# A graph layer with a gathered neighbour sum, linear attention and two experts: VectorE's large gather-stage steps take one SBUF operand, the last block's own products stand ahead of its last rows, the first expert is requested alone

## The chip, the core and the metric

The kernel runs on one core of one Trainium2 chip. A core has TensorE (PE, with its weight loads shown apart as PEld), VectorE (DVE), ScalarE (ACT), GpSimd (POOL) and SyncE (SP), an SBUF that all of them read, a PSUM of eight banks into which PE writes, and 16 DMA engines. The metric is the device time of one execution in microseconds (us).

## What is computed

```python
xn = layernorm(x)                                  # 12500 rows of 256
agg = segment_sum(xn[src], dst) / max(count, 1)    # 212500 edges, sorted by dst
gnn = relu(agg @ W_l.T + b_l + xn @ W_r.T) + xn
q, k, v = xn@wq+bq, xn@wk+bk, xn@wv+bv             # 8 heads of 32; q, k = elu(.) + 1
attn = (q (k^T v)) / (q . sum(k) + 1e-6) @ wo + bo
x1 = x + gnn + attn
y = layernorm(x1)
out = x1 + layernorm(y + top-2-of-8 experts(y)) * gamma + beta   # one choice for all rows
```

All of it is float32; biases and gains are drawn away from 0 and 1.

## The kernel before, in words

Each engine runs its own hand-ordered program, and they meet at counted semaphores. There are four stages.

**Table.** All rows of x are normalised and written to `xn_table` in HBM as two float16 parts, and the edge lists are turned into index and offset tables.

**Gather stage.** The 12500 output rows are 49 blocks of 256 rows. A block has 34 tiles of 128 edges (the last 29). For each tile POOL issues one indirect DMA that gathers 128 table rows into `msgs`, a ring of one block's tiles; VectorE compares an iota row with the edges' offsets (`one_hots`, L1504) and PE multiplies the one-hot by the gathered rows into a PSUM strip of `pa`. The tiles go in 8 batches per block of 4, 4, 5, 4, 4, 4, 5, 4. POOL may start a batch when ScalarE has copied its indices (`idx_ready`, L738, in ScalarE's order of work) and when PE has used the same batch of the block before (`batch_used`). Strips cover 128 rows and overlap by 64, so ScalarE takes them to SBUF (L768) and VectorE adds the lower and the upper halves of neighbours in `join_strips` (L1513, L1516), and makes a reciprocal count (L1520, L1522). ScalarE scales the joined strips by it (`scale_sums`, L775), and PE turns them (`turn_sums`, L1145).

Beside the gather runs the rest. In blocks 0 to 9 (`shadow_block`, `key_work`) it is the keys: rows turned (L982), `keys` in two halves into two PSUM banks (L995), a bias by VectorE (`add_bias`, L1378), an Exp, the feature map (L1386) and `add_keys` (L1005). In blocks 10 to 19 (`double_block`) two blocks' dense work goes with each gathered block, from block 20 on one (`stage3`; a hardware loop covers most). The dense work of a block: ScalarE normalises the rows (`block_xn`, L762), PE turns them (L1070), ScalarE copies them (L781), PE makes the queries (`queries`, L1078), ScalarE makes exp(q + bq) and q + bq + 1 in four activations (`block_queries`, L790 and L793), VectorE takes min and max (L1548), PE makes the normalizers (L1087), VectorE divides (`normalise_queries`: L1554, L1556, L1558), PE makes the sum's products in `base` (L1105, L1094, L1108, L1109), `mixed_product` and `neighbour_product` (L1094), ScalarE and VectorE finish the row (L800, L1537), its statistics follow, ScalarE makes y (`block_y`, L807), PE turns it (`turn_y`, L1134) and ScalarE keeps it (L815). ScalarE's order in a block's middle is: queries, `block_y`, then the index copies of batches 3 and 4 of the next block.

**Routing.** The mean of y gives the logits; a chain of tiny VectorE steps finds both experts, then SP reads the two numbers and requests W1, b1 and W2 of each.

**Experts.** Weights and y are split in a high and a low part; per quad of 512 rows PE runs `layer1` (L1275) and `layer2` (L1290).

## Time and profile before

| | |
|---|---|
| runs, median of 3 | 3372.62 us (3365.61 to 3381.5) |
| the profiled execution's own time | 3382.15 us |
| its span | 3380.7 us |
| mean granted TensorE clock | 0.809 of full speed |
| busy: PE, POOL, DVE, ACT | 2141.0, 1607.6, 1423.6, 955.7 us |
| gathers | 1661 indirect DMAs |

The profiled execution is 1.45 us longer than its span, and its span is what the rows below divide up. An engine's busy share is a mean over stages of unlike kind, so it says little here; the stages' windows say more.

### The profile page before, as it was taken

Reading aid. Unit: us, or ns where it says so; the run is one execution under the profiler, and the core shown is the slowest. Engines: PE = TensorE matmul, PEld = TensorE weight load, DVE = VectorE, ACT = ScalarE, POOL = GpSimd, SP = SyncE. Lnnn points to the kernel's source line nnn. Section 1 sums busy time; section 2 is a strip of 40 time slices with the busy share of each in tenths; the row PEclk is TensorE's granted clock in tenths of the full one; section 3 lists DMA queues with packets and bytes.
Section 4 is the critical chain, followed back from the end, with each engine's and each line's share of the span. In section 5 each row is a group of like instructions: output and inputs, shape, how many; then the busy total and the mean of one; then the engine's idle time right before and its main releaser. Section 6 shows DMA issues by size and latency. Waiting matters only on the chain.

```text
span 3380.7 us, 35327 instructions
## 1 busy us (share of the span) xinstructions
PE 2141.0 (63%) x10858; PEld 1625.9 (48%) x10858; DVE 1423.6 (42%) x3244; ACT 955.7 (28%) x2221; POOL 1607.6 (48%) x1679
## 2 busy tenths in 40 slices
PE   1147667657766775565465454654555557999998
PEld 0135445545444553343343333433333346999997
DVE  7612222334444443332333323333333335777777
ACT  4512222222222221111111111111111114656565
POOL 1256666665555555666566665666566640000000
PEclk9978788878777777767767777677777778999999
DMA  6633333333333333333333333333333322222221
GB/s 210 215 101 115 112 111 110 91 102 106 100 97 100 98 93 103 98 103 98 98 101 100 103 101 96 100 101 102 98 98 103 103 70 77 75 63 68 74 74 58
DMA packets 205191, 340.31 MB, mean 101 GB/s; under 512 B 33118, under 2 KB 151131, under 8 KB 205115
## 3 DMA queue, kind: packets, MB, share of 16 engines
q0 software_dynamic: 80160, 219.14, 22.6%
q1 hardware_dynamic: 124538, 119.81, 11.1%
q8 instruction: 42, 0.69, 0.1%
q10 hardware_dynamic: 416, 0.39, 0.1%
q14 instruction: 35, 0.28, 0.0%
HBM read 288.01 MB, written 51.20 MB: 100 GB/s over the span
## 4 chain that ended last, share of the span: by engine, by line
PE 41%; another core or an unknown queue 34%; issue 9%; ACT 7%; DVE 7%; DMA 1%; ACTq 1%; SPq 0%; DVEq 0%
PE pd L1290 8%; PE pd L1094 6%; PE pa L1275 4%; PE pc L1275 4%; PE pa L1244 3%; PE pd L995 2%; PE pa L1243 2%; PE pd L1105 2%; PE pd L1087 2%; PE pd L1134 1%; PE pc L1005 1%; PE pc L1145 1%; PE pd L1108 1%; PE pd L1109 1%
## 5 line engine op out<-in xcount | busy, mean ns | idle before, releaser
L672 POOL DMA_INDIRECT ring<-xn_table,idxb x1661 | 1598.8, 963 | 1150.4 <-issue 633.2
L1244 PE MATMUL pa<-ring,ohh 128*128 128x257 f16 x1661 | 472.0, 305 | 76.4 <-issue 76.2
L1243 PE MATMUL pa<-ring,ohh 128*128 128x256 f16 x1661 | 469.9, 304 | 75.0 <-issue 65.9
L1087 PE MATMUL pd<-work,KS_s 128*128 128x256 f32 x196 | 107.8, 652 | 472.3 <-DVE work L1548 395.5
L1290 PE MATMUL pd<-parts 128*128 128x256 f32 (+1 forms) x1568 | 312.2, 282 | 1.8 <-DVE parts L1747 1.8
L1087 PEld LDWEIGHTS pd<-work,KS_s 128*128 128x128 f32 x196 | 49.7, 313 | 489.0 <-DVE work L1548 404.6
L1244 PEld LDWEIGHTS pa<-ring,ohh 128*128 128x128 f16 x1661 | 179.8, 108 | 197.0 <-issue 121.8
L1094 PE MATMUL pd<-mats,work 128*128 128x256 f32 x784 | 260.1, 463 | 0.9 <-DVE work L1530 0.9
L1290 PEld LDWEIGHTS pd<-parts 128*128 128x128 f32 (+1 forms) x1568 | 253.1, 188 | 10.3 <-DVE parts L1747 2.4
L1504 DVE TENSOR_TENSOR ohh<-pc,edges 128x512 f16<-128x512 f32 (+1 forms) x307 | 214.2, 718 | 98.4 <-PE pa L1244 64.6
L768 ACT ACTIVATE ring<-pa 128x257 f32<-128x257 f32 x196 | 75.4, 385 | 620.1 <-remote 313.5
L1243 PEld LDWEIGHTS pa<-ring,ohh 128*128 128x128 f16 x1661 | 180.8, 109 | 129.3 <-issue 86.7
L1513 DVE TENSOR_TENSOR ring<-ring 64x514 f32<-64x514 f32 x49 | 33.5, 684 | 445.0 <-ACT ring L768 445.0
L1290 PE MATMUL pd<-W_lo_t,parts 128*128 128x256 f32 x784 | 219.7, 280 | 0.0
L1094 PEld LDWEIGHTS pd<-mats,work 128*128 128x128 f32 x784 | 164.2, 232 | 114.2 <-issue 91.7
L1548 DVE SCALAR_TENSOR_TENSOR work<-work 128x512 f32<-128x512 f32 x49 | 33.9, 692 | 425.3 <-ACT work L793 413.7
L790 ACT ACTIVATE work<-pd,bq_c 128x256 f32<-128x256 f32 x98 | 41.1, 471 | 535.0 <-remote 523.4
L995 PE MATMUL pd<-mats,yT 128*128 128x256 f32 x392 | 124.2, 472 | 103.0 <-ACT yT L723 102.5
L1145 PE MATMUL pc<-ident,ring 128*128 128x128 f32 x160 | 39.9, 397 | 209.1 <-ACT ring L775 209.1
L1556 DVE RECIPROCAL work<-work 128x512 f32<-128x512 f32 x49 | 164.3, 3353 | 1.7
L995 PEld LDWEIGHTS pd<-mats,yT 128*128 128x128 f32 x392 | 90.2, 242 | 128.9 <-ACT yT L723 112.8
L1290 PEld LDWEIGHTS pd<-W_lo_t,parts 128*128 128x128 f32 x784 | 147.2, 188 | 9.1
(205 smaller groups left out, 3726.1 us busy)
## 6 DMA issues: line engine op xcount, KB each, us to landing
ring<-xn_table,idxb POOLq DMA_INDIRECT x1661
yT<-in_x SPq DMA_DIRECT2D x48, 512.0 KB
xn_table<-ring SPq DMA_DIRECT2D x24, 512.0 KB, 5.4
x_rows<-work SPq DMA_DIRECT2D x48, 256.0 KB
y_rows<-work SPq DMA_DIRECT2D x48, 256.0 KB
work<-y_rows SPq DMA_DIRECT2D x24, 512.0 KB, 4.3
work<-x_rows SPq DMA_DIRECT2D x24, 512.0 KB, 3.7
out<-work SPq DMA_DIRECT2D x24, 512.0 KB, 3.1
```

The costliest lines, as they stand in the source:

```text
L672: pool.indirect_dma_start(out=msgs[:, k, 0:PARTS * D], out_offset=None, in_=xn_table[:, :], in_offset=bass.IndirectOffsetOnAxis(ap=idxb[:, ...
L768: nc.scalar.activation(strips[:, (NS * u + t + 1) % KEPT, 0:D + 1], pa[:, t % 2, 0:D + 1], ACT.Copy)\
L995: ins = mm(pd[0:n, 2 + pr, (t % 2) * D:(t % 2 + 1) * D], xTb[kq % 2][:, c, t * P:t * P + n], wk_s[:, c, :], start=c == 0, stop=c == C - 1)
L1087: ins = mm(pd[:, 0, c * BN:(c + 1) * BN], KS_s[:, c, :], pq[:, c * BN:(c + 1) * BN], start=True, stop=True)
L1094: ins = mm(pd[:, 2 + h, at:at + D], a[:, c * BN + h * P:c * BN + (h + 1) * P], w[:, c, :], start=False, stop=last and c == C - 1, skip_gro ...
L1145: ins = nc.tensor.transpose(to[:, c * BN + g * P:c * BN + (g + 1) * P], strips[:, NS * u + 2 * g + 1, c * P:(c + 1) * P], ident[:, :])
L1243: mm(pa[:, t % 2, 0:D], oh[:, slot, :], msgs[:, k, 0:D], start=begins, stop=False, skip_group_check=True)
L1244: ins = mm(pa[:, t % 2, 0:D + 1], oh[:, slot, :], msgs[:, k, D:2 * D + 1], start=False, stop=ends, skip_group_check=True)
L1275: ins = mm(hbank(f)[:, 0:w], wp[:, e, c, fc * P:(fc + 1) * P], yp[u][:, c, 0:w], start=c == 0 and wp is W1_hi and yp is y_hi, stop=c == C ...
L1290: ins = mm(pd[0:n, 2 * u + t // 2, (t % 2) * D:(t % 2 + 1) * D], hp[:, t * P:t * P + n], wp[:, f, :], start=f == 0 and t % 2 == 0 and hp i ...
L1504: V.tensor_tensor(oh[:, slot:slot + m, :], bc(row[:, c0:c0 + WIN], m), where, ALU.is_equal)\
L1556: V.reciprocal(qb, qb).then_inc(s["nrm_rec"], 1)
```

## The change

What the diff does, part by part:

- **One-hots of blocks 0 to 9**: the iota row is read from PSUM bank 3 of `pd` and no longer from SBUF. To free that bank, both halves of a quad's keys go to bank 2, so the second half waits for the bias step of the first, and stands one tile later, as do its `add_keys`.
- **Strip join**: VectorE adds only the counts (tiny). ScalarE scales each own strip, and also the neighbours' halves, by the same reciprocal, into a new buffer `mixed`. `turn_sums` multiplies both by the identity and lets PSUM add them: eight products for four.
- **Queries**: the bias enters as one product more of one row (`bq_r`, with 1 added) for each half. ScalarE then needs one activation of 512 columns for the four; VectorE reads the other operand from PSUM. The division runs in PSUM, and `turn_xn` waits for its end.
- **Last block** (29 tiles): both normalizers and the first `base` stand at tile 21, the second at tile 25; before, the normalizers stood at 24 and 25 and both bases behind the last tile.
- **Experts**: the first index is handed over before the second is looked for, its W1 comes in two halves, and they are split one after the other.

```diff
 def scale_sums(d, u):
     act.wait_ge(s["cnt_rec"], d + 1)
+    wait(act, s["agg_made"], d)
     for g in range(2):
         own = strips[:, NS * u + 2 * g + 1, 0:D]
-        ins = nc.scalar.activation(own, own, ACT.Copy, scale=cnts[:, g:g + 1])
+        nc.scalar.activation(own, own, ACT.Copy, scale=cnts[:, g:g + 1])
+    for part, n, g in other_halves(d, u):
+        ins = nc.scalar.activation(mixed[part, g, :], strips[part, n, 0:D], ACT.Copy, scale=cnts[part, g:g + 1])
...
 def block_queries(b):
-    for c in range(C):
-        nc.scalar.activation(pq[:, c * BN:(c + 1) * BN], pd[:, 1, c * BN:(c + 1) * BN], ACT.Exp, bias=bq_c[:, c:c + 1])
-    for c in range(C):
-        ins = nc.scalar.activation(qb[:, c * BN:(c + 1) * BN], pd[:, 1, c * BN:(c + 1) * BN], ACT.Identity, bias=bq1_c[:, c:c + 1])
-    ins.then_inc(s["eq_made"], 1)
+    nc.scalar.activation(pq, pd[:, 1, :], ACT.Exp, bias=minus1[:, :]).then_inc(s["eq_made"], 1)
...
 def keys(kq, pr, b):          # pr 0 and 1 now share bank 2
     if pr == 0:
         pe.wait_ge(s["xt_made"], kq + 1)
-    else:
         wait(pe, s["agg_taken"], b if kq > KEYS_OF[b][0] else b - 1)
+    else:
+        pe.wait_ge(s["kb_made"], 2 * kq + 1)
...
 def queries(d, o):
     for c in range(C):
-        ins = mm(pd[:, 1, o * BN:(o + 1) * BN], wq_s[:, c, o * P:(o + 1) * P], xT2[...], start=c == 0, stop=c == C - 1)
+        mm(pd[:, 1, o * BN:(o + 1) * BN], wq_s[:, c, o * P:(o + 1) * P], xT2[...], start=c == 0, stop=False)
+    ins = mm(pd[:, 1, o * BN:(o + 1) * BN], bq_r[0:1, o * P:(o + 1) * P], ones[0:1, :]..., start=False, stop=True)
...
 def turn_sums(d, u, to):
-    for g in range(2):
-        for c in range(C):
-            ins = nc.tensor.transpose(to[...], strips[:, NS * u + 2 * g + 1, c * P:(c + 1) * P], ident[:, :])
+    for c in range(C):
+        for g in range(2):
+            mm(o, strips[:, NS * u + 2 * g + 1, at_c], ident[:, :], start=True, stop=False)
+            ins = mm(o, mixed[:, g, at_c], ident[:, :], start=False, stop=True)
...
+LAST_BASE = (21, 25)          # last block: normalizers and base 0 at tile 21, base 1 at 25
...
 def one_hots(b, q):
-    row = iota_f[:, :] if isinstance(b, int) and NBT * b + q < NBT * DELAY + 4 else pc[:, 0, :]
+    row = pd[:, 3, :] if isinstance(b, int) and NBT * b + q < NBT * DELAY + 4 else pc[:, 0, :]
...
 def join_strips(d, u):
-    V.tensor_tensor(own[low, :, 0:D + 1], own[low, :, 0:D + 1], strips[low, NS * u:NS * u + 3:2, 0:D + 1], ALU.add)
-    for g in range(1 if last else 2):
-        V.tensor_tensor(own[high, g, 0:D + 1], own[high, g, 0:D + 1], strips[high, (NS * u + 2 * g + 2) % KEPT, 0:D + 1], ALU.add)
+    for part, n, g in other_halves(d, u):
+        ins = V.tensor_tensor(cnts[part, g:g + 1], strips[part, NS * u + 2 * g + 1, D:D + 1], strips[part, n, D:D + 1], ALU.add)
...
 def query_features(b):
-    V.scalar_tensor_tensor(out=pq, in0=pq, scalar=1.0, in1=qb, op0=ALU.min, op1=ALU.max)
+    V.scalar_tensor_tensor(out=pq, in0=pq, scalar=1.0, in1=pd[:, 1, :], op0=ALU.min, op1=ALU.max)
...
+V.tensor_copy(pick[:, 0:1], row(R_I, 1)).then_inc(s["picked"], 1)    # behind the first first_at
...
-V.tensor_copy(pick[:, :], row(R_I, 2)).then_inc(s["picked"], 1)
+V.tensor_copy(pick[:, 1:2], row(R_I, 1, 1)).then_inc(s["picked"], 1)
```

`other_halves` lists the neighbours' halves: four (partitions 0 to 63 or 64 to 127 of one strip), three in the last block.

## Rows read from the trace of the kernel before

**Rows 1.** Busy time by stage: start:end, length, engines, clock, DMA.

```profile
142.00:704.00 562.00, 341.50 (x1717) 264.87 (x1718) 144.75 (x243) 136.07 (x308) 365.17 (x375) 0.81 0.37 108
704.00:1301.00 597.00, 431.03 (x1844) 295.30 (x1843) 261.02 (x568) 150.72 (x433) 327.23 (x341) 0.79 0.34 100
1301.00:2666.00 1365.00, 730.10 (x3339) 502.26 (x3338) 446.59 (x938) 227.69 (x728) 846.49 (x884) 0.73 0.34 100
```

**Rows 2.** The page: chain of waits that ended last, by engine.

```profile
PE 41%; another core or an unknown queue 34%; issue 9%; ACT 7%; DVE 7%; DMA 1%; ACTq 1%; SPq 0%; DVEq 0%
```

**Rows 3.** POOL's timeline: start, us, instruction, idle time before it.

```profile
2011.08 0.95 POOL L672 DMA_INDIRECT ring<-xn_table,idxb  x1 [0.30 <-issue]
...
2030.82 1.32 POOL L672 DMA_INDIRECT ring<-xn_table,idxb  x1 [3.76 <-issue]
...
2058.47 0.95 POOL L672 DMA_INDIRECT ring<-xn_table,idxb  x1 [6.30 <-ACT idxb L738]
```

**Rows 4.** POOL's gathers, 142 to 704, then 1301 to 2666: count, busy, mean ns, idle.

```profile
L672 POOL DMA_INDIRECT ring<-xn_table,idxb x375 | 365.8, 975 | 328.9 <-issue 140.4 <-DMA xn_table<-ring 132.3 <-PE pa L1244 31.8
...
L672 POOL DMA_INDIRECT ring<-xn_table,idxb x884 | 846.7, 958 | 518.8 <-issue 344.2 <-ACT idxb L738 159.8 <-PE pa L1244 9.3
```

**Rows 5.** The chain that ended last, 2003 to 2060: start, us, what.

```profile
2012.53 12.55 another core or an unknown queue
...
2039.95 14.98 another core or an unknown queue
```

**Rows 6.** ScalarE's timeline, 2053 to 2059.

```profile
2054.95 0.84 ACT L790 ACTIVATE work<-pd,bq_c 128x256 f32<-128x256 f32 x2 [14.45 <-remote]
...
2056.39 1.10 ACT L807 ACTIVATE work<-work,nmr,rstd 128x256 f32<-128x256 f32 x2
```

**Rows 7.** ScalarE's groups by shape, 1301 to 2666: count, busy, mean ns.

```profile
L790 ACT ACTIVATE work<-pd,bq_c 128x256 f32<-128x256 f32 x52 | 21.8, 471 | 352.1 <-remote 347.5 <-PE pd L1078 4.5
...
L781 ACT ACTIVATE work<-pd 128x512 f32<-128x512 f32 x26 | 15.5, 597 | 23.2 <-remote 19.1 <-PE pd L1070 2.3 <-issue 1.2
```

**Rows 8.** VectorE's timeline, 2002 to 2033.

```profile
2011.56 0.69 DVE L1558 TENSOR_TENSOR work<-work 128x512 f32<-128x512 f32 x1
...
2030.63 0.69 DVE L1513 TENSOR_TENSOR ring<-ring 64x514 f32<-64x514 f32 x1 [16.43 <-ACT ring L768]
2031.35 0.77 DVE L1516 TENSOR_TENSOR ring<-ring 64x257 f32<-64x257 f32 x2
...
2032.35 0.17 DVE L1522 RECIPROCAL cnts<-cnts 128x2 f32<-128x2 f32 x1
```

**Rows 9.** PE's timeline in a block of the double stage.

```profile
989.88 1.03 PE L1078 MATMUL pd<-work,mats 128*128 128x256 f32 x4
...
1011.58 0.60 PE L1145 MATMUL pc<-ident,ring 128*128 128x128 f32 x4
```

**Rows 10.** ScalarE's timeline behind it.

```profile
997.95 0.84 ACT L790 ACTIVATE work<-pd,bq_c 128x256 f32<-128x256 f32 x2 [9.32 <-remote]
...
1002.67 0.91 ACT L775 ACTIVATE ring<-ring,cnts 128x256 f32<-128x256 f32 x2 [3.15 <-DVE cnts L1522]
```

**Rows 11.** PE at the end of the gather stage, timeline.

```profile
2776.67 0.70 PE L1087 MATMUL pd<-work,KS_s 128*128 128x256 f32 x2 [1.38 <-DVE work L1548]
...
2779.27 1.12 PE L1105 MATMUL pd<-blo_b,ones 1*128 1x512 f32 x2
...
2782.25 1.12 PE L1105 MATMUL pd<-blo_b,ones 1*128 1x512 f32 x2
...
2786.86 0.60 PE L1145 MATMUL pc<-ident,ring 128*128 128x128 f32 x4
```

**Rows 12.** Routing to the first expert product, timeline of all engines.

```profile
2802.74 0.15 DVE L1689 TENSOR_REDUCE ring<-ring 1x1 f32<-1x8 f32 x1
...
2804.36 0.16 DVE L1696 CAST ring<-ring 1x2 int32<-1x2 f32 x1
...
2812.96 1.19 PE L1275 MATMUL pa<-parts 128*128 128x512 f32 x2 [6.90 <-DVE W_lo_t L1719]
```

More of the change, by code:

```diff
@@ L947, in _ @@
             split_y(0, 0)
-            for e in range(2):
-                act.wait_ge(s[f"w1_loaded{e}"], 32)
-                nc.scalar.activation(W1_hi[:, e, :, :], W1_s[:, e, :, :], ACT.Copy).then_inc(s["w1_hi_made"], 1)
+            for e, loaded, count, fs in W1_PIECES:
+                act.wait_ge(s[loaded], count)
+                nc.scalar.activation(W1_hi[:, e, :, fs], W1_s[:, e, :, fs], ACT.Copy).then_inc(s["w1_hi_made"], 1)
             def normalise_z(q, u):
@@ L1065, in turn_xn @@
                 pe.wait_ge(s["xn2_ready"], d + 1)
-                wait(pe, s["nrm_eps"], d)
+                wait(pe, s["qhat_made"], d)
                 for h in range(2):
@@ L1077, in queries @@
                 for c in range(C):
-                    ins = mm(pd[:, 1, o * BN:(o + 1) * BN], wq_s[:, c, o * P:(o + 1) * P],
-                             xT2[:, c * BN:(c + 1) * BN], start=c == 0, stop=c == C - 1)
+                    mm(pd[:, 1, o * BN:(o + 1) * BN], wq_s[:, c, o * P:(o + 1) * P],
+                       xT2[:, c * BN:(c + 1) * BN], start=c == 0, stop=False)
+                ins = mm(pd[:, 1, o * BN:(o + 1) * BN], bq_r[0:1, o * P:(o + 1) * P], ones[0:1, :].unsqueeze(1).to_broadcast([1, 2, P]), start=False, stop=True)
                 if o == C - 1:
@@ L1164, in dense @@
                     base(b, BASE.index(k), u)
-                if k in DENSE:
+                if is_int(b, NB - 1) and k in LAST_BASE:
+                    if k == LAST_BASE[0]:
+                        for c in range(C):
+                            normalizers(b, c)
+                    base(b, LAST_BASE.index(k), u)
+                elif k in DENSE and not (is_int(b, NB - 1) and k > LAST_BASE[0]):
                     work, part, back = DENSE[k]
@@ L1175, in key_work @@
                         turn_rows(kq)
-                    if k in (o + 3, o + 4):
-                        keys(kq, k - o - 3, b)
-                    if k in (o + 7, o + 8):
-                        add_keys(kq, k - o - 7)
+                    if k in (o + 3, o + 5):
+                        keys(kq, (k - o - 3) // 2, b)
+                    if k in (o + 7, o + 9):
+                        add_keys(kq, (k - o - 7) // 2)
                 if k == 10 and b > 0:
                     pe.wait_ge(s["kb_made"], 2 * KEYS_OF[b][0] + 2)
-                    turn_sums(b - 1, 1 - u, pd[:, 3, :])
+                    turn_sums(b - 1, 1 - u, pd[:, 2, :])
             def double_work(b, k, u):
@@ L1247, in stage3 @@
                         ins.then_inc(s["batch_used"], 1)
-                if last_block:
-                    for h in range(2):
-                        base(b, h, u)
             for b in range(2 * DELAY):
@@ L1507, in join_strips @@
             def join_strips(d, u):
-                low, high = slice(0, STRIP), slice(STRIP, P)
-                own = strips[:, NS * u + 1:NS * u + 4:2, :]
                 last = is_int(d, NB - 1)
                 dve.wait_ge(s["strip_taken"], NS * d + (NS if last else NS + 1))
-                V.tensor_tensor(own[low, :, 0:D + 1], own[low, :, 0:D + 1], strips[low, NS * u:NS * u + 3:2, 0:D + 1], ALU.add)\
-                    .then_inc(s["halves_added"], 1)
-                for g in range(1 if last else 2):
-                    V.tensor_tensor(own[high, g, 0:D + 1], own[high, g, 0:D + 1],
-                                    strips[high, (NS * u + 2 * g + 2) % KEPT, 0:D + 1], ALU.add)\
-                        .then_inc(s["halves_added"], 1)
-                dve.wait_ge(s["halves_added"], 3 * d + (2 if last else 3))
-                V.tensor_scalar(cnts[:, :], own[:, :, D], 1.0, XS, ALU.max, ALU.mult).then_inc(s["cnt_max"], 1)
+                wait(dve, s["strips_scaled"], d)
+                if last:
+                    dve.wait_ge(s["agg_made"], d)
+                    V.memset(mixed[HIGH, 1, :], 0.0)
+                    V.tensor_copy(cnts[HIGH, 1:2], strips[HIGH, NS * u + 3, D:D + 1])
+                for part, n, g in other_halves(d, u):
+                    ins = V.tensor_tensor(cnts[part, g:g + 1], strips[part, NS * u + 2 * g + 1, D:D + 1],
+                                          strips[part, n, D:D + 1], ALU.add)
+                ins.then_inc(s["halves_added"], 1)
+                dve.wait_ge(s["halves_added"], d + 1)
+                V.tensor_scalar(cnts[:, :], cnts[:, :], 1.0, XS, ALU.max, ALU.mult).then_inc(s["cnt_max"], 1)
                 dve.wait_ge(s["cnt_max"], d + 1)
@@ L1547, in query_features @@
                 dve.wait_ge(s["eq_made"], b + 1)
-                V.scalar_tensor_tensor(out=pq, in0=pq, scalar=1.0, in1=qb, op0=ALU.min, op1=ALU.max)\
+                V.scalar_tensor_tensor(out=pq, in0=pq, scalar=1.0, in1=pd[:, 1, :], op0=ALU.min, op1=ALU.max)\
                     .then_inc(s["phq_made"], 1)
@@ L1739, in _ @@
             split_w1(0)
+            split_w1(1)
             split_w2(0)
```

85 lines of the change are left out of this document (48 added, 37 removed).

## The prediction

> **What bounds the kernel.** I began with the busy time by stage [rows 1]. The table stage and the experts are touched only at their edges; 2524 us of the span are the gather stage, in three stretches: 562 us for ten blocks with the keys, 597 us for ten blocks with two dense blocks each, 1365 us for 26 blocks with one. No engine is busy all the time in any of them. The reader should next look at the one engine that cannot be helped: POOL issues 1661 gathers, and where nothing stops it they follow each other every 1.25 us (0.95 us busy, 0.30 us between [rows 3]). That is 42.6 us for 34 tiles, and in the last stretch a block takes 1365 / 26 = 52.5 us. The difference lies in two stops per block. One is 3.76 us long, before the batch that waits for PE's use of the old one; the other is 6.30 us, before a batch whose indices ScalarE has not copied [rows 3]. 3.76 + 6.30 less twice the usual 0.30 is 9.5 us, which with 42.6 and the long gather below makes 52.4 us. So the last stretch is POOL's rate plus two stops, and of these the second follows ScalarE's program.
>
> Then I read the chain that ended last, and this is where my forecast is weakest. The page gives 34% of it to "another core or an unknown queue" [rows 2], though there is one core. The pieces are 12.55 and 14.98 us long and end where ScalarE at last sees PE's products [rows 5], while PE's own records have these products long done. In the double stretch PE's records of the queries end at 990.9 [rows 9] and ScalarE takes them at 997.95 after 9.32 us of idling [rows 10]; in the last stretch this wait is 14.45 us [rows 6] and 352 us in all, over 52 activations, two a block, so 26 blocks [rows 7]. Nothing that I read says what holds PE's results back in there. It bears on every edit that gives PE more to do before ScalarE may go on.
>
> **The queries.** Removed: four activations. They start at 2054.95, and `block_y` behind them at 2056.39, so they hold ScalarE for 1.44 us [rows 6]. Added: one of 128x512 from PSUM, as the copy at L781, 0.60 us [rows 7]. ScalarE is 0.84 us earlier at `block_y` and so at the index copies for which POOL stands still, so this is on the path: -0.84 us. Added before it: one product of one row and 256 columns per half. The trace has a one-row product of 512 columns (L1105), no one of 256; four full products with 256 columns take 1.03 us [rows 9], 0.26 each. Bounds: 0, if both are done before the hold-up ends, and, as PE is held up there, 14.45 us / 8 products = 1.8 us each. I take one of the two on the path at 0.26 us, since the row of such products is nearer than a quotient of a wait. VectorE's min and max with one operand in PSUM I leave at the price of the SBUF form (0.69 us is what 512 columns cost it in either kind of work [rows 8]); the same for the division, whose 3 steps are covered by tiles of the next block before anyone asks for them. The new wait of `turn_xn` on the division's end is met: the division ends with L1558 at 2012.25 [rows 8], and the turn comes behind a join at 2030.63.
>
> **The join.** Removed on VectorE: from 2030.63 to 2032.52, 1.89 us [rows 8]. Added: four sums of one column and the same two count steps, each like L1522 at 0.17 us plus a hand-over, 1.2 us together: -0.7 us. Added on ScalarE: four activations of 256 columns on half the partitions; L775 does two on all partitions in 0.91 us [rows 10], so 0.46 each, and I assume that half the partitions save nothing: +1.84 us (lower bound half of it). Added on PE: a second pass of four turns, +0.60 us [rows 9]. Together `turn_sums` ends 1.7 us later. In the last stretch POOL is already running again by then (2030.82 [rows 3]) and the next thing it can wait for is 20 us away, behind the hold-up, so I cost it at nothing; if that cover is gone it is 1.7 us a block, 45 us in all. The queued index copy behind `scale_sums` is for batch 2 of the next block, eleven gathers or more away.
>
> **Gather and VectorE.** The gather that begins at 2030.82 overlaps L1513 and L1516 and takes 1.32 us in place of 0.95, and ends just where L1516 ends [rows 3, 8]. L1558, also with two SBUF operands, lies over the gather of 2011.08, which takes the usual 0.95 [rows 3, 8]. So the edit is worth 0.37 us a block here. In the key stretch the mean is 975 ns against 958 in the last stretch [rows 4] and 949 for a plain gather (0.95 [rows 3]): 26 ns times 375, 9.8 us at most. There POOL has many stops, so I count half, -5 us, between 0 and -9.8.
>
> The Trainium skill speaks on both sides (page "SBUF — State Buffer", section "Who interferes with whom"): a VectorE instruction with two SBUF inputs contends with a GpSimd instruction that reads SBUF, but the page also holds that writing descriptors is not what such an instruction blocks. Its first sentence would price the whole overlap, 1.46 us a block instead of 0.37, its second 0; the trace shows a value between them, at one place of two. By the second the sum below would be 15 us smaller in gain.
>
> **The sum, on the profiled execution of 3382.15 us.** Last stretch: 26 x (0.84 + 0.37 - 0.26) = -24.7 us. Key stretch: -5 us; the second half of the keys now waits for VectorE's bias of the first, one tile later, which I leave at nothing, as PE waits there for others anyway, with up to +2 us a block (20 us) as its upper bound. Double stretch: here the period is a chain through PE, ScalarE and VectorE, since POOL waits for PE. A block has two dense blocks: activations 2 x -0.84, query products 4 x 0.26, one join -0.7, +1.84, +0.60: +1.1 us, ten blocks, +11 us. End of the gather stage: before, normalizers begin at 2776.67 and the last `turn_sums` ends at 2787.46, with two bases of 2.98 us behind the last tile [rows 11]. After, the bases stand ahead of tiles 21 and 25: base, four tiles (0.9, a guess by the 0.26 of such a product), base, four tiles and a turn (1.4, likewise) end the tiles at 2777.4 + 2.98 + 0.9 + 2.98 + 1.4 = 2785.7; then a strip copy and VectorE's counts (1.4 by guess), five activations (2.3) and eight turns (1.2) end at 2790.6, +3.1 us, as the sums now stand behind the last row alone, plus 1.7 us from the join of the block before. Less 0.7 us each from the two blocks outside the loop: +3.4 us. Experts: the first index was complete at 2802.89 and was handed over at 2804.52 [rows 12]; with half a matrix to load and split, PE may begin some 3 us before 2812.96, but the first Gelu stands behind all three splits on ScalarE, so I count -2 us. Sum: -24.7 - 5 + 11 + 3.4 - 2 = -17.3 us. The execution of 3382.15 us is 9.5 us above the median, and I carry the difference over: 3372.6 - 17.3, about 3355 us.
>
> **Rivals.**
>
> *The added products pay the hold-up's price (slower).* If each product that stands before a hand-over costs what the held-up ones do, 9.32 us / 8 = 1.17 us in the double stretch, four a block cost 4.7 us instead of 1.0: +37 us. If in the last stretch the turns, late by 1.7 us, fall into the hold-up, the queries come as much later: +45 us. One alone gives 3392 to 3400 us, both 3437. For it: rows 5, 7 and 10. Against it: in the last stretch the hold-up ends close to where POOL stops, whatever PE has left. It decides from a gain of 17 us lost, 0.7 us per block over 26 blocks.
>
> *It cancels (same).* Gathers get no relief, as the one of 2011.08 shows no harm [rows 3] (-9.6 and -5 fall away), and ScalarE's 1.84 us reach the path in a fifth of the 26 late blocks (+9): -17.3 + 14.6 + 9 = +6, so 3365 to 3380 us. The first half of this is what that page of the Trainium skill says in its second sentence.
>
> *The hold-up shrinks too (faster).* It is longest where VectorE and POOL both work; if one-operand steps shorten it by a tenth in the last stretch, 35 us of the 352 [rows 7] go: 3320 us. Against it: VectorE idles for 12 us in the midst of a hold-up (a 16.43 us idle stretch ends at 2030.63 [rows 8]).
>
> **Chances.** The sum as worked out 0.40 (3338 to 3370; about 0.28 of it below the bound), the shrinking hold-up 0.10, cancelling 0.22, slower 0.28. A difference of 0.5%, 17 us, is about what a measurement here can tell from none. Faster: 0.28 + 0.10 = 0.38. Same: 0.12 + 0.22 = 0.34. Slower: 0.28. The range reaches from 3325, leaving out most of the big gain, to 3412, which takes in one of the two slow mechanisms.
>
> **What would show it.** Right: late blocks of 51.5 us; the second stop 5.7 us; no gather of 1.3 us; ScalarE's L790 successor x1 a block at about 0.6 us; double blocks about 1 us longer; the last turn of sums later against the last gather; the first expert product 2 to 3 us nearer to the routing. Wrong: the wait of the Exp for the queries above 14.45 us in the last stretch or above 9.32 us in the double one (the slow rival), a third stop of POOL in a late block, or double blocks shorter than before, which would mean that the removed activations and VectorE steps count for more on the chain than the products put in.

## The result, and the profile after

The changed kernel took 3402.54 us (median of 20 runs, 3370.29 to 3438.21), the kernel before 3369.83 us (20 runs, 3354.91 to 3381.5): a ratio of 1.0086, with a 95% interval of 1.0065 to 1.0108. By this ratio it is slower by 29 us (the two medians differ by 33) where I had forecast 17 us faster; the time lies within the stated range, on the other side of the kernel before. It also scatters more: 68 us between its extremes, 27 us before.

The first thing to read is the chain of waits by engine, from the page of the changed kernel. It is much as it was [rows 2].

```profile
PE 45%; another core or an unknown queue 32%; ACT 8%; issue 7%; DVE 6%; DMA 1%; ACTq 0%; SPq 0%; POOL 0%; DVEq 0%; POOLq 0%
```

To see where the 31 us of the two profiled executions (3380.7 and 3411.9 us span) went, I took the start of each block's first gather from POOL's timeline. Between these starts:

| us | before | after | my sum said |
|---|---|---|---|
| key blocks 0 to 9 | 507.6 | 521.8 | -5 |
| double blocks 10 to 19 | 589.6 | 593.0 | +11 |
| late blocks 20 to 46 | 1426.8 | 1432.6 | -24.7 |
| blocks 47, 48 to the last gather | 91.9 | 99.7 | (in the end's +3.4) |
| last gather to the mean | 40.8 | 43.2 | +3.4 |
| mean to the first split of W1 | 13.8 | 10.2 | |
| from there to the end | 567.8 | 568.8 | -2 with the line above |

The span grew by 31.2 us where the sum had -17.3, so 48 us are to be found. Two lines are far off: the late blocks, 30 us worse than worked out, and the key blocks, 19 us worse. The end of the gather stage is 7 us worse and the double blocks are 8 us better. The windows between these starts (columns as in [rows 1]) show PE busier in each than before (318.20, 411.49 and 772.94 us over the same stretches of the kernel before), at much the same granted clock (0.82, 0.79 and 0.73 there):

```profile
142.00:664.00 522.00, 329.69 (x1696) 253.75 (x1697) 128.00 (x237) 148.44 (x326) 326.52 (x340) 0.84 0.36 107
664.00:1257.00 593.00, 456.31 (x1974) 310.04 (x1972) 236.48 (x532) 144.30 (x392) 321.45 (x341) 0.80 0.33 99
1257.00:2690.00 1433.00, 915.44 (x3945) 612.19 (x3945) 451.93 (x1027) 271.38 (x799) 867.65 (x919) 0.72 0.33 99
```

Each gather became as short as I had said. POOL's gathers over the late blocks, to be held against the second line of [rows 4] (958 ns there):

```profile
L689 POOL DMA_INDIRECT ring<-xn_table,idxb x919 | 868.5, 945 | 565.4 <-issue 356.5 <-ACT idxb L755 118.6 <-remote 76.0
```

But POOL's timeline over one late block shows three stops where there were two [rows 3]:

```profile
1998.29 0.94 POOL L689 DMA_INDIRECT ring<-xn_table,idxb  x1 [3.84 <-issue]
2015.17 0.94 POOL L689 DMA_INDIRECT ring<-xn_table,idxb  x1 [2.22 <-remote]
2025.84 0.94 POOL L689 DMA_INDIRECT ring<-xn_table,idxb  x1 [4.73 <-ACT idxb L755]
2050.66 0.94 POOL L689 DMA_INDIRECT ring<-xn_table,idxb  x1 [3.87 <-issue]
```

The stop behind ScalarE's queries fell by 1.57 us, from 6.30 to 4.73, where I had claimed 0.58 (0.84 less 0.26); the gather of 1.32 us is gone; and a new stop of 2.22 us, ahead of batch 2, takes it all back: 2.22 + 4.73 + 3.87 = 10.8 us a block, before 10.1 us and the long gather. The block stays at 52.4 us.

The new stop waits for PE's use of the old batch 2, which stands behind `turn_sums`. PE's record of its last tile ends at 2008.33, 10.0 us after POOL went on at 1998.29 (before: 2038.12, 7.3 us after 2030.82). That would still be in time for POOL, whose last gather ahead of the stop ends at 2012.96; but POOL goes on only at 2015.17. The first and last records of that turn, and ScalarE behind it (timelines of PE and ScalarE):

```profile
2002.37 0.79 PE L1163 MATMUL pc<-ident,ring 128*128 128x128 f32 x2 [5.28 <-issue]
...
2005.52 0.57 PE L1164 MATMUL pc<-ident,ring 128*128 128x128 f32 x2
...
2009.25 0.60 PE L1086 MATMUL pd<-ident,work 128*128 128x128 f32 x4
```

```profile
2014.40 0.39 ACT L785 ACTIVATE ring<-pa 128x257 f32<-128x257 f32 x1 [11.85 <-remote]
...
2015.90 0.60 ACT L802 ACTIVATE work<-pd 128x512 f32<-128x512 f32 x1 [0.15 <-remote]
2023.20 0.69 ACT L810 ACTIVATE work<-pd,minus 128x512 f32<-128x512 f32 x1 [6.70 <-PE pd L1096]
2023.79 1.08 ACT L822 ACTIVATE work<-work,nmr,rstd 128x256 f32<-128x256 f32 x2
```

The turn ends at 2006.09, 7.8 us after POOL went on at 1998.29. Before, it ended at 2034.70, 3.9 us after POOL had gone on at 2030.82 [rows 3]; its record in PE's timeline:

```profile
2033.59 1.11 PE L1145 MATMUL pc<-ident,ring 128*128 128x128 f32 x4 [6.03 <-ACT ring L775]
```
In both traces PE's results still come at once for a while from there, and then no more until POOL has stood still. Before, the turned rows came through (PE's record ends 9.1 us after POOL went on, and ScalarE takes them at once, at 2039.90) and only the queries were caught (12.0 us after; ScalarE takes them at 2054.95). After, the turned rows are caught as well: PE's record ends at 2009.85, 11.6 us after POOL went on, and ScalarE takes them at 2015.90, 2.9 us after POOL's last gather has ended. What ScalarE then needs for the queries, 0.59 us from their start to `block_y`, is the 0.84 us less that I had worked out.

### The profile page after: what moved, and what is told of

Its sections match the earlier page's. It is cut to its first block, busy times and chain, and to the rows that moved or that the text cites. A ratio compares the mean times of both kernels' runs of the same rounds, so it can differ in the third digit from the quotient of the medians.

```text
span 3411.9 us, 37092 instructions
## 1 busy us (share of the span) xinstructions
PE 2358.2 (69%) x11642; PEld 1751.7 (51%) x11642; DVE 1386.7 (41%) x3298; ACT 1007.5 (30%) x2270; POOL 1583.9 (46%) x1679
## 4 chain that ended last, share of the span: by engine, by line
PE 45%; another core or an unknown queue 32%; ACT 8%; issue 7%; DVE 6%; DMA 1%; ACTq 0%; SPq 0%; POOL 0%; DVEq 0%; POOLq 0%
PE pd L1311 8%; PE pd L1111 5%; PE pa L1296 4%; PE pc L1296 4%; PE pa L1268 3%; PE pa L1267 3%; PE pd L1094 3%; PE pd L1011 3%; PE pd L1122 2%; ACT ring L795 2%; PE pd L1096 2%; PE pc L1021 2%; PE pd L1104 2%; PE pd L1126 1%
## 5 line engine op out<-in xcount | busy, mean ns | idle before, releaser
L689 POOL DMA_INDIRECT ring<-xn_table,idxb x1661 | 1575.1, 948 | 1205.6 <-issue 629.2
L1268 PE MATMUL pa<-ring,ohh 128*128 128x257 f16 x1661 | 491.9, 313 | 100.1 <-issue 99.8
L1094 PE MATMUL pd<-work,mats 128*128 128x256 f32 x392 | 154.9, 535 | 168.2 <-ACT work L802 149.9
L1111 PE MATMUL pd<-mats,work 128*128 128x256 f32 x784 | 234.6, 426 | 5.4 <-DVE work L1554 5.2
L1163 PE MATMUL pc<-ident,ring 128*128 128x128 f32 x320 | 98.4, 407 | 196.5 <-ACT ring L795 132.0
L1540 DVE TENSOR_TENSOR cnts<-ring 64x1 f32<-64x1 f32 x195 | 31.2, 160 | 413.3 <-ACT ring L785 411.3
L1094 PEld LDWEIGHTS pd<-work,mats 128*128 128x128 f32 x392 | 94.3, 266 | 196.3 <-ACT work L802 163.0
L1163 PEld LDWEIGHTS pc<-ident,ring 128*128 128x128 f32 x320 | 79.7, 306 | 219.0 <-issue 151.1
L1580 DVE RECIPROCAL pd<-pd 128x512 f32<-128x512 f32 x49 | 164.9, 3366 | 1.7
L1561 DVE TENSOR_TENSOR work<-work,pd 128x512 f32<-128x512 f32 x49 | 33.7, 687 | 285.3 <-ACT work L815 213.1
```

Of the source, the lines that this page charges most:

```text
L689: pool.indirect_dma_start(out=msgs[:, k, 0:PARTS * D], out_offset=None, in_=xn_table[:, :], in_offset=bass.IndirectOffsetOnAxis(ap=idxb[:, ...
L1094: mm(pd[:, 1, o * BN:(o + 1) * BN], wq_s[:, c, o * P:(o + 1) * P], xT2[:, c * BN:(c + 1) * BN], start=c == 0, stop=False)
L1111: ins = mm(pd[:, 2 + h, at:at + D], a[:, c * BN + h * P:c * BN + (h + 1) * P], w[:, c, :], start=False, stop=last and c == C - 1, skip_gro ...
L1163: mm(o, strips[:, NS * u + 2 * g + 1, at_c], ident[:, :], start=True, stop=False)
L1268: ins = mm(pa[:, t % 2, 0:D + 1], oh[:, slot, :], msgs[:, k, D:2 * D + 1], start=False, stop=ends, skip_group_check=True)
L1580: V.reciprocal(pd[:, 0, :], pd[:, 0, :]).then_inc(s["nrm_rec"], 1)
```

## The experiments

The kernels ran in five groups; those of one group ran on one chip, and share its runs of the kernel before. One thing must be known ahead: in the first three groups (chips 10, 9 and 8) the kernel before took 2859 to 2862 us and not 3370, while in the last two (chip 10 again) it took 3368 to 3372. I call the first condition calm and the second held; the profiled pair is held. A ratio is always taken within one group.

### What each part is worth in the calm condition

`join_undone`:

```diff
-    for part, n, g in other_halves(d, u):        # six activations, eight products
+    V.tensor_tensor(own[low, ...], own[low, ...], strips[low, ...], ALU.add)   # as before: the halves in SBUF,
+    ins = nc.tensor.transpose(to[...], strips[...], ident[:, :])               # two activations, four transposes
```

> The changed kernel with the strip join as it was (VectorE adds the halves in SBUF, two activations, four transposes). Theory 1, the turn by products is mis-priced: the sixteen passes of 0.21 us end the turn 2.9 us later than four transposes and cause the third stop of a late block (3.0 us, before batch 2). Then without them the third stop goes, late blocks fall from 52.4 to about 51 us, and the whole kernel is 20 to 35 us faster than the changed one, that is, near or below the kernel before. Rival, the late block's length is set by how long PE's results are held back and not by what is added: blocks stay at 52.4 to 52.5 us with two stops in place of three, and the whole is within 8 us of the changed kernel.

Measured 2840.86 us, ratio 0.9932 (0.9910 to 0.9953). Its late blocks took 42.8 us, POOL's own rate, without the stops of the profiled pair, so this run can't say what the join does to those stops.

`keys_undone`:

```diff
-    row = pd[:, 3, :] if isinstance(b, int) and NBT * b + q < NBT * DELAY + 4 else pc[:, 0, :]
+    row = iota_f[:, :] if isinstance(b, int) and NBT * b + q < NBT * DELAY + 4 else pc[:, 0, :]
-    mm(pd[0:n, 2, ...], xTb[kq % 2][...], wk_s[:, c, :], ...)       # both halves in bank 2
+    mm(pd[0:n, 2 + pr, ...], xTb[kq % 2][...], wk_s[:, c, :], ...)
```

> The changed kernel with blocks 0 to 9 as they were (iota row from SBUF, keys in two PSUM banks, no extra wait). The key stretch took 507.7 us before and 521.8 after. Theory 1, the wait of the second half of the keys on the bias of the first costs 1.4 us a block: the stretch returns to about 508 us, the whole is 10 to 15 us faster than the changed kernel. Rival, the loss there is one chance stop of 10.3 us in block 5 and comes with neither: the stretch is 508 to 515 us here and also in the other kernels that keep the edit.

Measured 2862.46 us, 1.0002 (0.9993 to 1.0012); key blocks 437.6 us.

`queries_undone`:

```diff
-    nc.scalar.activation(pq, pd[:, 1, :], ACT.Exp, bias=minus1[:, :])
+    for c in range(C): nc.scalar.activation(pq[...], pd[:, 1, ...], ACT.Exp, bias=bq_c[:, c:c + 1])
+    for c in range(C): nc.scalar.activation(qb[...], pd[:, 1, ...], ACT.Identity, bias=bq1_c[:, c:c + 1])
```

> The changed kernel with the queries as they were (four activations, bias by ScalarE, no bias products, division in SBUF). Theory 1, the edit is a small gain where ScalarE is waited for: late blocks 0.5 to 1.0 us longer than 52.4, the whole 10 to 25 us slower than the changed kernel. Rival, the two bias products take 0.62 us each and not 0.26, 1.24 us a block, more than the 0.84 us that ScalarE gains: the whole is 0 to 15 us faster than the changed kernel.

Measured 2864.11 us, 1.0009 (0.9997 to 1.0020).

`turn_by_products`:

```diff
-    ins = nc.tensor.transpose(to[...], strips[:, NS * u + 2 * g + 1, c * P:(c + 1) * P], ident[:, :])
+    ins = mm(to[...], strips[:, NS * u + 2 * g + 1, c * P:(c + 1) * P], ident[:, :], start=True, stop=True)
```

> The kernel before, with the four transposes of the joined strips made as four products with the identity, nothing else. The turn then takes 1.7 us and not 0.6. Theory 1, the turn lies on the path of a late block, as PE does it before the tiles whose batches POOL waits for: late blocks 0.5 to 1.1 us longer, whole 15 to 35 us slower. Rival, the turn is covered in late blocks: late blocks at 52.5 us, whole within 6 us of the kernel before.

Measured 2862.74 us, 1.0006 (0.9996 to 1.0016): in the calm condition PE's longer turn alone is covered, as the rival had it. The condition was new, so I ran both kernels and two parts alone in the next group. `before_again` and `changed_again` are the two kernels unchanged; `join_alone` and `queries_alone` are the kernel before with that part of the change's diff.

> The kernel before once more, for its trace beside that of the others. In the four runs so far POOL hardly ever stopped, blocks took 43 us and the whole 2862 us, where the profiled run of before had two stops per late block and 3382 us. If what held PE's results back belongs to the chip or the moment and not to the kernel, this run has late blocks of about 43.1 us, no stop over 0.5 us in them, and a span near 2860 us; if the edits of the four kernels removed it, it has blocks of 52.5 us.

> The changed kernel itself. By adding up the four runs (undoing the keys or the queries left 2862 and 2864 us, undoing the join 2841 us) it should stand at 2855 to 2865 us here, within 0.3% of the kernel before. If the loss of 0.86% was owed to the held-back results alone, it is equal or faster here; if it is owed to the added work, it is again 20 us or more slower.

> The kernel before with the new join and nothing else: counts alone on VectorE, six activations, eight products with the identity. Theory 1, the join is the part that costs: 15 to 30 us slower than before, in the double stretch and the end, as the turn takes 3.4 us for 0.6 and ScalarE 2 us more. Rival, the join costs only together with the queries' bias products: within 6 us of the kernel before.

> The kernel before with the new queries and nothing else. Theory 1, a bias product of 0.6 us per half and the saving on ScalarE about cancel: within 6 us of the kernel before. Rival, the shorter queries are a gain in the double stretch, where the chain through ScalarE sets the period: 8 to 20 us faster.

Measured: `before_again` 2860.99 us in one run; `changed_again` 2851.94 us, 0.9971 (0.9961 to 0.9982), so here the change is a small gain; `join_alone` 2874.04 us, 1.0045 (1.0029 to 1.0062), so the join is a part that costs; `queries_alone` 2849.96 us, 0.9964 (0.9952 to 0.9977), a gain of the size of its rival, but in the late blocks and not in the double ones, as the table below shows.

The chain of waits of `before_again`, by engine, has no unknown part, and in its timeline the last queries of a block and the Exp behind them lie where they should:

```profile
POOL 39%; PE 35%; issue 14%; DVE 5%; ACT 3%; DMA 3%; POOLq 1%; SPq 0%; ACTq 0%; DVEq 0%
```

```profile
1638.33 1.03 PE L1078 MATMUL pd<-work,mats 128*128 128x256 f32 x4
...
1639.39 0.84 ACT L790 ACTIVATE work<-pd,bq_c 128x256 f32<-128x256 f32 x2 [2.31 <-PE pd L1078]
```

PE's products end at 1639.36 and ScalarE starts at 1639.39; in [rows 9, 10] the same step took from 990.9 to 997.95. The kernel is the same, so the 34% of [rows 2] is a condition and no property of the program. Stretches by the same starts as above, in the calm condition:

| us | key | double | late 20 to 46 | last gather to mean | span |
|---|---|---|---|---|---|
| before_again | 436.7 | 431.7 | 1161.0 | 28.0 | 2859.5 |
| changed_again | 430.8 | 447.0 | 1152.9 | 26.6 | 2856.0 |
| join_undone | 430.2 | 428.5 | 1154.3 | 22.1 | 2832.8 |
| keys_undone | 437.6 | 446.1 | 1153.0 | 26.5 | 2861.1 |
| queries_undone | 431.8 | 441.0 | 1160.6 | 28.4 | 2861.5 |
| join_alone | 437.7 | 444.3 | 1160.1 | 32.6 | 2877.8 |
| queries_alone | 436.3 | 430.7 | 1153.5 | 26.4 | 2848.5 |
| y_first (below) | 431.8 | 426.0 | 1150.2 | 26.5 | 2831.6 |

Down a column each edit can be read off, from one profile of each kernel: the iota row in PSUM is worth 6 us in the key blocks, the queries 8 us in the late blocks, and the join costs 13 to 19 us in the double blocks and 4 to 5 us at the end. The parts don't simply add: with the join in, the queries cost 6 us in the double blocks (441.0 to 447.0), without it nothing (431.7 and 430.7).

### Where the join costs in the double blocks

In ScalarE's order there, `scale_sums` stands ahead of `block_y`. Timelines of ScalarE and PE in a double block of `changed_again`:

```profile
928.78 0.91 ACT L793 ACTIVATE ring<-ring,cnts 128x256 f32<-128x256 f32 x2 [2.32 <-DVE cnts L1546]
929.59 2.05 ACT L795 ACTIVATE ring<-ring,cnts 64x256 f32<-64x256 f32 x4
931.66 1.09 ACT L822 ACTIVATE work<-work,nmr,rstd 128x256 f32<-128x256 f32 x2
```

```profile
932.81 0.66 PE L1151 MATMUL pd<-ident,work 128*128 128x128 f32 x4 [4.00 <-ACT work L822]
...
935.26 2.08 PE L1111 MATMUL pd<-mats,work 128*128 128x256 f32 x4
```

PE waits 4.00 us for y, and afterwards runs at the lower clock (the four records at 935.26 take 2.08 us, 1.13 us at the higher; the granted clock is 1.00 of full speed from 929 to 933 us and 0.62 from 933 to 937.3). Three kernels ask whether it is this order or PE's own work. `y_first`:

```diff
-    if half == 0: scale_sums(b - 1, 1 - u)
     if d > 0: block_y(d - 1)
+    if half == 0: scale_sums(b - 1, 1 - u)
```

`join_no_products` is `join_alone` with the old four transposes; `eight_products` is the kernel before with the new turn, both products from the same strip; `best` is `join_undone` with the order of `y_first`.

> The changed kernel with ScalarE's block_y ahead of scale_sums in the double blocks. There block_y now stands behind VectorE's counts and six activations, and PE waits for its y. Theory 1, this is how the join costs 15 us in the double stretch (447.0 us against 431.7 before): the stretch returns to 431 to 436 us and the whole is 11 to 16 us faster than the changed kernel (2852), near 2838 us. Rival, it is PE's products that fill the half: the stretch stays above 442 us, the whole within 5 us of 2852.

> join_alone with the four transposes in place of the eight products: all of ScalarE's and VectorE's part of the join stays, the neighbours' halves are left out of the sum. join_alone had 444.3 us in the double stretch and 32.6 us from the last gather to the mean, before 431.7 and 28.0. Theory 1, in the double stretch ScalarE's order costs and not PE: 441 to 445 us there. Rival, the products cost: 431 to 434 us there.

> The kernel before with eight products with the identity in place of the four transposes (each strip taken twice, so the sums come out doubled); VectorE and ScalarE as before. Theory 1: PE's 2.8 us more per block are within the slack of a double block, which POOL bounds at 43 us: 431 to 436 us in the double stretch, whole 2860 to 2868 us. Rival, PE is the bound of the double stretch: 441 us or more there, whole 2872 us or more.

> All of the change but the join, and block_y ahead of scale_sums in the double blocks. join_undone stood at 0.9932 of before with a double stretch of 428.5 us, three stops of 1.3 us in it. If block_y behind the join is what delays PE there, these stops go and the whole is 2 to 4 us faster than join_undone, about 0.992 of before; if not, it stays at 0.993.

Measured: `y_first` 2829.37 us, 0.9886 (0.9867 to 0.9905); `join_no_products` 2858.4 us, 0.9989 (0.9975 to 1.0003), double blocks 433.6 us; `eight_products` 2862.76 us, 1.0005 (0.9995 to 1.0015), double blocks 430.2 us; `best` 2830.54 us, 0.9894 (0.9875 to 0.9913), double blocks 426.1 us. So neither PE's eight products nor ScalarE's six activations cost much there alone (430.2 and 433.6 us, 431.7 before), against my first theory for `join_no_products`; together they do, and taking `block_y` out from behind them removes the cost altogether. `y_first` came out 9 us faster than expected, with 426.0 us for the double blocks where I had allowed 431 to 436. `best` stands 10 us below `join_undone` by the ratios of two groups, where its double blocks gained 2.4 us (428.5 to 426.1). The windows of the double blocks of `changed_again` and of `y_first`:

```profile
573.00:1020.00 447.00, 395.57 (x1887) 271.98 (x1887) 232.38 (x531) 139.92 (x377) 321.44 (x341) 0.91 0.45 131
```

```profile
572.00:998.00 426.00, 395.73 (x1999) 274.62 (x2000) 245.63 (x567) 149.62 (x404) 322.35 (x341) 0.96 0.48 140
```

426 us is ten times the 42.6 us of POOL's own rate: nothing is left to gain there, and the granted clock is up from 0.91 to 0.96.

### The held condition

> The kernel before with block_y ahead of scale_sums in the double blocks and nothing else. Theory 1, the order costs only with the long join: before is bound by POOL there (431.7 us for ten blocks, no stop), so the stretch stays at 430 to 432 us and the whole within 3 us of before. Rival, the order is a gain of its own: 427 us or less, whole 4 us or more faster.

> The changed kernel with block_y ahead of scale_sums in the double blocks, again, beside the changed kernel on one chip: 0.987 to 0.990 of before, double stretch 426 us, if the first measurement stands.

> The changed kernel, again. Where PE's results come at once it stands at 0.996 to 0.998 of before with a double stretch of 447 us; where they are held back, at 1.006 to 1.011 with three stops per late block.

`order_alone` is the kernel before with the order of `y_first`; `y_first_2` and `changed_third` are `y_first` and the changed kernel again. In this group the condition of the profiled pair was there: `order_alone` 3346.77 us, 0.9899 (0.9864 to 0.9935); `y_first_2` 3374.29 us, 0.9994 (0.995 to 1.0037); `changed_third` 3423.44 us, 1.0145 (1.0059 to 1.0231). The expectation for `order_alone` was made for the calm condition, in which it was never run; in the held one the order is a gain of its own, 25 us, as its rival had it. `y_first_2` missed its 0.987 to 0.990, which held for the calm condition alone, but is 49 us faster than `changed_third` beside it; `changed_third` lies above its 1.006 to 1.011, with an interval that takes them in. Three parts followed, as `join_undone`, `join_alone` and `queries_alone`:

> All of the change but the join, where PE's results are held back. Theory 1, the join alone makes the third stop and the stops of 13 us: late blocks have two stops again, the second 5.5 us and not 6.3, no block over 55 us, 51.2 to 51.7 us a block; whole 0.98 to 0.992 of before. Rival, the queries' bias products or the wait for the division do it: three stops or 13 us stops remain, whole 0.998 or more. If results come at once: 0.993, as measured.

> The join alone, where PE's results are held back. Theory 1: third stop, or single stops near 13 us, in the late blocks as in the changed kernel; whole 1.008 to 1.02 of before. Rival: late blocks as before with two stops, whole within 0.5% of before. If results come at once: 1.0045, as measured.

> The queries alone, where PE's results are held back. Theory 1: two stops, the second 5.5 us for 6.3, whole 0.985 to 0.997 of before. Rival, each bias product pays the hold-up's price: the second stop longer than 6.3 us, whole 1.005 or more. If results come at once: 0.9964, as measured.

Measured: `join_undone_2` 3359.22 us (four runs, 3316 to 3372; before 3367.74), without an interval, so inconclusive as a whole; `join_alone_2` 3353.27 us, 0.9972 (0.994 to 1.0003); `queries_alone_2` 3333.34 us, 0.9899 (0.9837 to 0.996), as its first theory said. The stretches, from one profile of each:

| us | key | double | late 20 to 46 | last gather to mean | span |
|---|---|---|---|---|---|
| before | 507.6 | 589.6 | 1426.8 | 40.8 | 3380.7 |
| after | 521.8 | 593.0 | 1432.6 | 43.2 | 3411.9 |
| changed_third | 502.7 | 578.9 | 1450.4 | 49.5 | 3408.6 |
| y_first_2 | 528.1 | 546.1 | 1436.8 | 43.8 | 3371.3 |
| order_alone | 503.0 | 545.2 | 1424.8 | 41.3 | 3335.6 |
| join_undone_2 | 551.9 | 536.0 | 1399.8 | 46.0 | 3345.6 |
| join_alone_2 | 514.4 | 604.0 | 1370.0 | 45.9 | 3346.8 |
| queries_alone_2 | 505.7 | 570.7 | 1410.6 | 41.7 | 3344.1 |

POOL's stops in two late blocks of `join_undone_2`, two a block as before, the second of 5.6 us in place of 6.3, and with the old join the long gather of 1.32 us is back:

```profile
1666.91 0.94 POOL L689 DMA_INDIRECT ring<-xn_table,idxb  x1 [5.47 <-ACT idxb L755]
1691.65 1.32 POOL L689 DMA_INDIRECT ring<-xn_table,idxb  x1 [3.79 <-issue]
1718.61 0.94 POOL L689 DMA_INDIRECT ring<-xn_table,idxb  x1 [5.63 <-ACT idxb L755]
```

In the changed kernel some blocks have a single long stop in place of the second and third: 4 of 27 in `changed_third`, 58.7 us each. Its POOL, and ScalarE ahead of it:

```profile
1575.19 0.94 POOL L689 DMA_INDIRECT ring<-xn_table,idxb  x1 [12.97 <-ACT idxb L755]
1599.96 0.94 POOL L689 DMA_INDIRECT ring<-xn_table,idxb  x1 [3.78 <-issue]
```

```profile
1565.24 0.60 ACT L802 ACTIVATE work<-pd 128x512 f32<-128x512 f32 x1 [5.80 <-remote]
1572.54 0.69 ACT L810 ACTIVATE work<-pd,minus 128x512 f32<-128x512 f32 x1 [6.70 <-PE pd L1096]
```

Here batch 2 was free just in time, POOL ran on to the end of its indices at 1562.2, and only then, 3 us later, did the turned rows come through, with the queries (6.70 us at the lower clock) and y still to do. And `join_alone_2` has a third pattern, with no stop of 3.8 us ahead of batch 7:

```profile
2077.19 0.94 POOL L680 DMA_INDIRECT ring<-xn_table,idxb  x1 [4.47 <-remote]
2089.22 0.94 POOL L680 DMA_INDIRECT ring<-xn_table,idxb  x1 [2.33 <-remote]
2096.21 0.94 POOL L680 DMA_INDIRECT ring<-xn_table,idxb  x1 [1.04 <-ACT idxb L746]
2114.16 0.94 POOL L680 DMA_INDIRECT ring<-xn_table,idxb  x1 [2.93 <-remote]
```

Its blocks are 48.2 and 52.4 us by turns, and its late stretch is the shortest of all, 57 us under that of before, while its double stretch is 14 us longer. That goes against my theory that the join alone makes the loss: in the late blocks it is the join together with the queries' edit.

## Why the prediction was wrong, step by step

**The late blocks, the step that failed.** The sum had -24.7 us there, measured is +5.8. It put the later turn of the sums at nothing, because "the next thing it can wait for is 20 us away, behind the hold-up". The rest of that line was near: without the join (`join_undone_2`) the late blocks fall by 27.0 us. That this is so close to 24.7 is partly luck, since the long gather and its 9.6 us stay there; the usual block fell from 52.5 to 51.7 us, 0.8 against 0.58 for the queries, and 7 us of the 27 are in the first late block alone. What the join adds was mis-sized and mis-placed. The second pass of the turn was priced at 0.60 us, as four transposes. It is not a pass of transposes: all eight are products of float32 data, and take 3.5 us together (PE's timeline at the end of the gather stage, against 0.60 us for the last line of [rows 11]):

```profile
2817.97 0.55 PE L1163 MATMUL pc<-ident,ring 128*128 128x128 f32 x2 [2.87 <-ACT ring L795]
...
2820.87 0.63 PE L1164 MATMUL pc<-ident,ring 128*128 128x128 f32 x2
```

So the turn ends 3.9 us later in the block (7.8 for 3.9), not 1.7 us: some 1.3 us of it are VectorE's and ScalarE's part, which I had at 1.1, and 2.6 us are PE's (3.72 for 1.11), which I had at 0.6. That is enough for the next hand-over, the turned rows, to be caught too. The traces show it in nearly every late block. Counted from where POOL goes on behind its stop ahead of batch 7, in blocks 21 to 46 with that stop:

| us | turn of the sums ends | turned rows end | ScalarE takes them more than 2.2 us later |
|---|---|---|---|
| before | 3.8 to 4.3 | 7.9 to 9.6 | in 1 block of 25 |
| join_undone_2 | 3.8 to 5.0 | 8.0 to 10.6 | in 5 of 25 |
| after | 7.5 to 8.9 | 11.2 to 13.3 | in all 26, by 4.3 to 12.7 |

Together with the queries' edit this gives the three stops or the single one of 13 us: 1432.6 and 1450.4 us. It is the second half of the slow rival ("the turns ... fall into the hold-up"), which gave +45 us for the late blocks; measured are 33 and 51 us between `join_undone_2` and the changed kernel's two profiles. Of the signs named, the third stop of POOL came; the Exp's wait did not grow but fell, from 14.45 to 6.70 us, since now an earlier hand-over is caught. The rival's first half did not come: the double blocks are 3 us longer and not 48. Its price per product was also misread: the eight records ahead of the Exp are four products. That the same join alone makes the late blocks shorter shows that such terms can't be added in the held condition: a hand-over is either ahead of the point or behind it. Why `join_alone_2` has no stop ahead of batch 7 I have not settled. Nor did any kernel take the join's activations and its products apart in the held condition; by the durations the products are two thirds of the delay.

**Key blocks.** -5 us was right where nothing else stops POOL: 436.7 to 430.8 us, calm. In the held condition the four profiles with the edit have 502.7 to 551.9 us, the four without it 503.0 to 514.4 us. The long ones have POOL stops of 9 to 11 us ahead of single batches. Ahead of batch 1 the stops of blocks 1 to 9 add up to 22 to 59 us with the edit and 14 to 22 us without it. I had allowed up to +20 us for the wait of the second half of the keys. In block 5 of `join_undone_2` the long stop does stand behind it (timelines of PE, VectorE and POOL):

```profile
397.71 3.78 PE L1007 MATMUL pd<-mats,yT 128*128 128x256 f32 x8 [4.42 <-DVE yT L1394]
...
408.86 0.69 DVE L1394 TENSOR_TENSOR yT<-pd,yT 128x512 f32<-128x512 f32 x1 [11.20 <-remote]
...
416.97 0.94 POOL L689 DMA_INDIRECT ring<-xn_table,idxb  x1 [10.52 <-PE pa L1263]
```

PE waits 4.42 us for the bias of the first half, the second half ends at 401.49, and VectorE takes it 7.4 us later, once POOL has stopped. So here too a hand-over came later and was caught. That is one block; `changed_third` has the edit and no such stop, and no kernel undid the edit alone in the held condition, so how much of the 19 us is this wait stays open.

**Double blocks.** +11 us was near: +15.3 us calm, +3.4 us in the pair. But the reason was not the sum of durations. It is `block_y` behind the join's activations on ScalarE and PE's 4.00 us for it: the order alone is worth 21 us of the changed kernel's double blocks when calm (447.0 to 426.0) and 33 to 47 us when held, and 44 us with the old join (`order_alone`, 589.6 to 545.2 us). In the held condition part of this is chance, as two profiles of the changed kernel differ by 14 us there. So the nearness of +11 is luck. I listed what the join adds to ScalarE and did not name what is queued behind it.

**Queries.** The saving of 0.84 us on ScalarE was right (1.44 us before [rows 6], 0.59 us after). A bias product costs 0.6 us and not 0.26. I had read the four records of [rows 9] as four products, but each product makes two records; and both bias products stand ahead of the Exp:

```profile
2799.99 0.69 PE L1096 MATMUL pd<-ones,work 1*128 1x256 f32 x2
```

The part as a whole is a gain in both conditions, 0.9964 and 0.9899.

**The join's other terms.** VectorE's part and ScalarE's are as worked out: the four sums begin at 2050.47 and the reciprocal ends at 2051.80, 1.3 us for 1.9, and the four activations on half the partitions take 2.05 us, so half the partitions saved nothing.

```profile
2050.47 0.71 DVE L1540 TENSOR_TENSOR cnts<-ring 64x1 f32<-64x1 f32 x4 [16.19 <-ACT ring L785]
...
2051.63 0.17 DVE L1546 RECIPROCAL cnts<-cnts 128x2 f32<-128x2 f32 x1
```

**Gathers.** 0.37 us a block was right: the mean fell by 13 ns, and by 34 that is 0.44 us. The Trainium skill's first sentence (page "SBUF — State Buffer", section "Who interferes with whom") holds to this extent: the step with two SBUF operands lengthened one gather of two that it met, and without such steps the gathers over 1.1 us fell from 71 to 14 in the profiled pair, and from 91 (`before_again`) to 16 (`changed_again`). Its second sentence, that writing descriptors is not blocked, is not decided here: a gather also reads its indices from SBUF (`idxb`), and no run takes the two apart.

**End of the gather stage and experts.** The bases ahead of the last rows are a gain: 22.1 us from the last gather to the mean in `join_undone`, 26.4 in `queries_alone`, which lacks them. I had only looked at what the end loses, +3.4 us, with eight turns at 1.2 us that take 3.5. Calm the change gains 1.4 us there (28.0 to 26.6); in the profiled pair the end with blocks 47 and 48 lost 10.2 us, most of it ahead of the last gather. The first expert was requested earlier as said; in the routing's timeline the first index is complete at 2836.97 and its request follows at 2837.92:

```profile
2836.83 0.14 DVE L1715 CAST ring<-ring 1x1 int32<-1x1 f32 x1
...
2837.92 0.41 SPq L630 DMA_DIRECT2D mats<-in_L_ffn_W  x1
...
2843.30 1.19 PE L1296 MATMUL pa<-parts 128*128 128x512 f32 x2 [3.29 <-DVE W_lo_t L1745]
```

The first split, now of half a matrix, is done 3.6 us sooner against the mean, and 1.0 us of it is lost in the experts: -2.6 us, for -2.

## What to carry to other kernels

Where a chain of waits has a large unknown part, take the kernel's profile more than once, on another chip and at another time, before you price anything against it: here it was a condition in which the same kernel takes 3370 or 2860 us. When an edit makes a step longer, name the instruction that is queued behind it on its own engine; moving `block_y` ahead of `scale_sums` took the changed kernel from 0.9971 to 0.9886 of before when calm, and the kernel before to 0.9899 when held, where of the change's own parts only the queries were worth as much (0.9899). And a product with the identity is not priced as a transpose.

## What the runs showed of the hardware

- The held condition. PE's records have a product done, and the engine that waits for it goes on later: by 11 to 13 us for the queries in nearly all late blocks of the kernel before, and once, early in its key blocks, by 37 us (the turned rows end at 164.59 and ScalarE takes them at 201.55). In the late blocks this is mostly 2.8 to 3.0 us after POOL's last gather has ended; the gathers themselves keep their 1.25 us. In `before_again` both hand-overs take 0.04 us at most. The condition was there in the profiled pair and in two groups of runs on chip 10, and absent in one group on the same chip 10 and on chips 8 and 9, with the kernel before unchanged. It costs 18% of the time. Its cause is open; no kernel here could bring it about or take it away.
- Eight products of 128x128 float32 with the identity take 3.5 us, four transposes 0.60 us; at the higher clock they follow each other every 0.43 and every 0.11 us.
- A float32 product of one row and 256 columns makes two records, as a full one does, and the two take 0.69 us; the four records of two full products of the queries take 1.03 us. So one row is not cheaper than 128.
- ScalarE's activation of 256 columns of float32 in SBUF takes 0.50 us on 64 partitions and 0.50 us on 128 (means over the whole kernel after, L795 and L793).
